# First attention of a macaron block: score products of the two-head fills on 32-row strips

## The reference

```python
Q = to_heads(x @ Wq); K = to_heads(x @ Wk); V = to_heads(x @ Wv)   # 16 heads of 8 features
scores = jnp.einsum('bhqd,bhkd->bhqk', Q, K) * scale
scores = jnp.where(causal_mask, -1000000.0, scores)
weights = jax.nn.softmax(scores, axis=-1)
attn = jnp.einsum('bhqk,bhkd->bhqd', weights, V)
```

## Time and profile before

| what | value |
|---|---|
| three runs, median (lowest to highest) | 2415.77 us (2415.32 to 2420.69) |
| profiled execution, its time | 2419.18 us |
| its span from the first to the last instruction | 2417.4 us |
| mean granted TensorE clock | 0.965 |
| busy: PE, PEld, DVE, ACT, POOL | 2228.5, 1476.6, 1759.1, 1448.1, 947.4 us |
| score products by query, 512 (L675): PE first and last start | 414.1 and 804.0 us |
| score products by key, 512 (L697): PE first and last start | 429.4 and 818.2 us |

### The profile page before, as it was taken

The page is one execution under the profiler, slowest core; times in us unless marked ns, Lnnn a source line. Parts: engine busy times, 40 slices in busy tenths (PEclk is TensorE's granted clock), DMA queues, the critical chain, the costliest instruction groups (busy, mean ns, idle before and its releaser), DMA issues.

```text
span 2417.4 us, 46156 instructions
## 1 busy us (share of the span) xinstructions
PE 2228.5 (92%) x11168; PEld 1476.6 (61%) x11168; DVE 1759.1 (73%) x3588; ACT 1448.1 (60%) x2256; POOL 947.4 (39%) x903
## 2 busy tenths in 40 slices
PE   2999998999999989999999999998989889999999
PEld 2666666666666666666667777763323337676666
DVE  4676675766777567666678887876767787778887
ACT  3655654554555555656576766665556556666666
POOL 1554454222232345555544444442121234444443
PEclk9999999999999999999999999998989899999999
DMA  3000002233222000000000000012323200000000
GB/s 144 1 0 0 0 0 61 62 89 96 85 78 72 16 12 13 13 9 11 14 1 1 0 0 0 0 46 78 105 78 99 83 1 5 5 4 4 4 4 9
DMA packets 59566, 78.93 MB, mean 33 GB/s; under 512 B 22784, under 2 KB 27104, under 8 KB 59232
## 3 DMA queue, kind: packets, MB, share of 16 engines
q1 hardware_dynamic: 59488, 77.99, 10.6%
HBM read 48.08 MB, written 29.88 MB: 32 GB/s over the span
## 4 chain that ended last, share of the span: by engine, by line
PE 55%; issue 17%; DVE 12%; POOL 11%; ACT 2%; DVEq 1%; DMA 1%; POOLq 0%; SPq 0%; ACTq 0%
PE pair L371 11%; POOL h_lo L1277 10%; PE pair L373 9%; PE pair L372 9%; PE pair L754 3%; PE bank L574 3%; PE pair L675 3%; PE pair L697 3%; PE bank L560 3%; PE pair L574 3%; PE pair L656 1%; PE bank L371 1%; DVE rmax L1110 1%; PE pair L684 1%; PE bank L373 1%
## 5 line engine op out<-in xcount | busy, mean ns | idle before, releaser
L1283 POOL TENSOR_TENSOR h_lo<-hid,h_hi 128x512 fp32r<-128x512 f32 x256 | 349.6, 1366 | 505.6 <-ACT h_hi L842 505.4
L1277 POOL TENSOR_TENSOR h_lo<-hid,h_hi 128x512 fp32r<-128x512 f32 x272 | 351.4, 1292 | 365.5 <-ACT h_hi L804 364.7
L371 PE MATMUL pair<-xnT_hi,w_hi 128*128 (+1 forms) x1056 | 484.4, 459 | 2.0 <-POOL w_lo L1275 1.2
L836 ACT ACTIVATE hid<-pair,bias 128x512 f32<-128x512 f32 x512 | 352.0, 688 | 181.5 <-PE pair L373 165.9
L372 PE MATMUL pair<-xnT_lo,w_hi 128*128 (+1 forms) x1056 | 421.6, 399 | 0.0
L373 PE MATMUL pair<-xnT_hi,w_lo 128*128 (+1 forms) x1056 | 420.3, 398 | 0.0
L371 PE MATMUL pair<-h_hi,w_hi 128*128 128x512 f32 x784 | 328.5, 419 | 40.6 <-DVE h_lo L1052 26.2
L372 PE MATMUL pair<-h_lo,w_hi 128*128 128x512 f32 x784 | 311.7, 398 | 0.0
L373 PE MATMUL pair<-h_hi,w_lo 128*128 128x512 f32 x784 | 311.7, 398 | 0.0
L1050 DVE CAST h_hi<-hid 128x512 fp32r<-128x512 f32 x256 | 193.1, 754 | 144.9 <-ACT hid L836 143.5
L804 ACT ACTIVATE h_hi<-hid 128x512 fp32r<-128x512 f32 x272 | 171.6, 631 | 176.5 <-DVE hid L1042 162.2
(11 more groups left out here) (177 smaller groups left out, 3669.3 us busy)
## 6 DMA issues: line engine op xcount, KB each, us to landing
parts_dram<-attn_parts SPq DMA_DIRECT2D x96, 256.0 KB, 2.9
attn_q_st<-parts_dram SPq DMA_DIRECT2D x64, 256.0 KB, 2.7
k_one<-parts_dram SPq DMA_DIRECT2D x128, 64.0 KB, 2.4
attn_k_st<-parts_dram SPq DMA_DIRECT2D x32, 256.0 KB, 3.0
stage_w<-in_w_dram SPq DMA_DIRECT2D x32, 130.0 KB, 2.1
stage_w<-in_w_dram SPq DMA_DIRECT2D x6, 512.0 KB, 12.6
x<-in_x_dram SPq DMA_DIRECT2D x1, 2048.0 KB, 7.8
mixed_dram<-attn_aT SPq DMA_DIRECT2D x32, 64.0 KB
```

The costliest lines, as they stand in the source:

```text
L371: eng.matmul(o, w_hi_, v_hi, start=start, stop=False, **kw)
L836: eng.activation(hid[:, j % NHID, :], bank[j % 3][:, :], ACT.Relu, bias=bias[:, B1 + j:B1 + j + 1]).then_inc(hid1_ready, 1)
L1277: eng.tensor_tensor(h_lo[:, p % NH0, :], hid[:, p % NHID, :], h_hi[:, p % NH0, :].bitcast(F32), ALU.subtract).then_inc(lo_ready, 1)
L1283: eng.tensor_tensor(h_lo[:, j % NH1, :], hid[:, j % NHID, :], h_hi[:, j % NH1, :].bitcast(F32), ALU.subtract).then_inc(lo1p_ready, 1)
```

## The change

A helper `strip(fill, j)` gives all 128 rows for fill 4 and the 32 rows of head j for fills 0 to 3. Both operands of both score products take these rows. The zeros of `k_one` are then not read in fills 0 to 3, and the result is the same sum. The numbers of instructions, their order, their waits and the banks that they write are as before; 12 of the 16 score products of a quad by query, and 12 of 16 by key, have 32 rows in place of 128, and the two heads of such a fill lie on neighbouring strips.

```diff
+        def strip(fill, j):
+
+            return slice(0, P) if fill == NF - 1 else slice(PC * j, PC * (j + 1))
+
         def scores_by_query(eng, ch, f, b):
...
             for j in heads_in(fill):
                 at0 = 256 * (j // 2) if fill == NF - 1 else 0
+                rows_ = strip(fill, j)
                 for i, (qt, at) in enumerate(Q_FILLS[fill][1]):
                     w, at = (qt + 1) * P, at + at0
-                    eng.matmul(pair[b][:, j % 2, at:at + w], mem0.q_st[:, quad, qt * P:(qt + 1) * P],
-                               mem0.k_one[:, quad, j, 0:w], start=(i == 0 and at0 == 0), stop=True, skip_group_check=True)
+                    eng.matmul(pair[b][:, j % 2, at:at + w], mem0.q_st[rows_, quad, qt * P:(qt + 1) * P],
+                               mem0.k_one[rows_, quad, j, 0:w], start=(i == 0 and at0 == 0), stop=True, skip_group_check=True)
...
         def scores_by_key(eng, ch, f, b):
...
             for j in heads_in(fill):
                 at0 = 256 * (j // 2) if fill == NF - 1 else 0
+                rows_ = strip(fill, j)
                 for i, (kb, at) in enumerate(K_FILLS[fill][1]):
                     w, at = S - kb * P, at + at0
-                    ins = eng.matmul(pair[b][:, j % 2, at:at + w], mem0.k_one[:, quad, j, kb * P:(kb + 1) * P],
-                                     mem0.q_st[:, quad, kb * P:S], start=(i == 0 and at0 == 0), stop=True, skip_group_check=True)
+                    ins = eng.matmul(pair[b][:, j % 2, at:at + w], mem0.k_one[rows_, quad, j, kb * P:(kb + 1) * P],
+                                     mem0.q_st[rows_, quad, kb * P:S], start=(i == 0 and at0 == 0), stop=True, skip_group_check=True)
             ins.then_inc(st_ready, 1)
```

## The result

The changed kernel takes 2466.70 us (median of four runs, 2463.44 to 2471.30), before 2415.55 us in the same comparison. The ratio is 1.0209, 95% interval 1.0187 to 1.0231: **slower by 51 us**. The prediction said 2486 us, slower, because TensorE's clock would fall in attn0. The page's row of busy times hides it: TensorE is busy 92% of the span as before, now of 2465.9 us.

What follows compares the result with a forecast made beforehand. TensorE's queue was taken to bound attn0. From the profiled 2419.2 us, -2 for the queue and +72 for the clock gave 2489, or 2486 us as a median; range 2412 to 2550.

Steps and rivals of the forecast that it cites:

- TensorE's queue bounds attn0: In attn0, TensorE's own queue sets the pace, except for one wait of up to 2.2 us for VectorE.
- wait of L704: TensorE's only large wait in attn0, once a chunk, read as for VectorE's maxima: 16.3 us in 370.
- Strips run side by side at full speed: From attn1's four 24-row products in 0.44 us: a two-product fill's second product runs beside the first, 0.23 us saved.
- Four-product fills, 0.12 us taken: Q2, Q3, K2 and K3 in attn0: each fill saves 0.12 us, 0.48 us a quad (0.16 to 1.16).
- case of program order: In a four-product fill, products start only in code order: 0.42 us in place of 0.57, 0.15 saved.
- upper bound of 0.29: In a four-product fill, the second head runs fully beside the first: 0.29 us saved of 0.57.
- Queue net -2 us: TensorE's queue in attn0: shape costs less strip gains, -4.5 us over 32 quads, half of gains taken: -13 to +6.
- Changes of shape: TensorE switching between strips and full rows: 0.09 us if a bf16 load follows, 0.18 if a float32r load follows.
- 1.26 us a quad: Cost in attn0 of switching between strips and full rows: 0.90 at fills plus 0.36 around inserted full-row steps.
- The clock holds less on few rows: A microsecond of products on few rows holds TensorE's clock up less than on all rows; forecast's chance 0.65.
- Its size, +72 us: Clock term in attn0: low-clock share 0.4 makes a chunk 58.6 us, +9.0, so +72 us for eight.
- ends of the clock term: Low-clock share 0.24, attn1's, gives +35 us; share 0.6 gives +128 us; stated as 2445 to 2550 us.

Runs made afterwards that it cites:

- three runs with full-row products at that place: Unread 512-column products added once a chunk: eight in the changed kernel, 2459.67 us; seven in the kernel before, 2431.73; seven with strips only in scores_by_query, 2418.30.
- By query alone: Changed kernel with scores_by_key back on all 128 rows, strips only in scores_by_query: 2415.36 us, ratio 0.9995 against the kernel before.
- 64-row run: Changed kernel with both heads of fills 0 to 3 on the 64 rows in which they lie: 2477.43 us, ratio 1.0266 against the kernel before.
- pair of extra products: Changed kernel plus eight unread 512-column products once a chunk at the same place: on 128 rows 2459.67 us, on 32 rows 2492.90 us.
- its halves: Changed kernel with strips kept only in scores_by_query, 2415.36 us, ratio 0.9995, or only in scores_by_key, 2428.77 us, ratio 1.0052, against the kernel before.
- tables of before: Unchanged step tables; other runs spread VectorE's steps to later slots: kernel before 2413.21 us, strips only in scores_by_query 2418.37, changed kernel 2453.32.
- K0 and K1 alone: Strips only in the two-product fills of scores_by_key, all other score products on 128 rows: 2418.58 us, ratio 1.0017 against the kernel before.

## Why the prediction was right, point by point

- **TensorE's queue bounds attn0.** Right: VectorE and ScalarE work as long as before, and a chunk follows TensorE's clock. The wait of L704 was misread in its cause: it is for the bank pair of Q0, not for the new maxima. The sum doesn't hang on that, but the three runs with full-row products at that place missed their forecasts with it.
- **Strips run side by side at full speed.** Right, from attn1's row, and across fills too, which the sum left out: at 630.33 four products on four strips, where the prediction has "at best two at a time".
- **Four-product fills, 0.12 us taken, near the case of program order.** The term was mis-sized: the fill takes 0.44 us to the mask instead of 0.57, with 0.09 for the change of shape in it, so 0.22 are saved, between the middle and the upper bound of 0.29. (The 0.04 of exposed load in these bounds has no row of its own.) Products of different strips overtake each other. The Trainium skill (TensorE: Matmul & The Clock Gate, Part 3) has products start in strict program order; the rows at 634.04 don't agree.
- **Queue net -2 us, bounds -13 to +6.** Carried back to full clock, 1.3 us a chunk, 10 us over eight chunks: near the lower bound. By query alone it is 1.0 to 1.3 us a chunk, measured at equal clock.
- **Changes of shape.** No run times one alone. That they cost something fits the 64-row run, 2.5 us a chunk with little gained, but the slower sequence of products on the same rows is in that too. The 1.26 us a quad stay unproven.
- **The clock holds less on few rows.** Right, and now shown by the pair of extra products, 33 us apart. The stretches of the earlier trace rows were weaker ground than the prediction took them for: the one of attn1 also holds products on column strips (1772.04 in the earlier trace rows). The Trainium skill (TensorE: Matmul & The Clock Gate, Part 1) has the clock follow how busy TensorE has been. By that the two runs of the pair would have the same clock; they have 0.83 and 0.74, and the measurement decides.
- **Its size, +72 us.** The share of the low clock in a chunk was taken as 0.4 and measured as 0.46; each microsecond of it was priced at 0.44 and costs 0.36; chunks at full clock take an estimated 47.1 us and not 48.3. A chunk takes 56.2 us and not 58.6: +6.6 and not +9.0, 53 us and not 72 for eight. That is about the 19 us by which the median was forecast too high. The errors cancel in part, and that is luck: by the prediction's own formula the larger share alone gives 16 us more, the lower price then takes some 21 off and the shorter chunk some 12. The price may be lower because part of the low clock lies over waits, which it doesn't lengthen; no run tests that. And the ends of the clock term, 2445 to 2550, should be 2449 to 2542 by their own terms; the measured time lies in both.
- **Open:** why the loss isn't the sum of its halves (0 and 13 us against 51). The traces show that low stretches last longer on few rows (13.7, 34.1 and 41.0 us at the start of the stage) and that, with the tables of before, only the two sets of strips together bring falls away from the long wait, four a chunk and not one. Why it takes both is open: no run puts a set number of strip products between full-row ones.

## What to carry to other kernels

A product whose unused rows are zero isn't only waste: here its full rows held TensorE's clock up. Before small products are packed on strips, read the granted clock of a stage that already does so, and count what the queue gains against what the clock gives back; packing only some of the products was neutral here (by query alone, or K0 and K1 alone) or cost little (7 to 13 us). And before filling a wait, find out which buffer it is for: work put behind it is only paid for.

## What was unexpected in the hardware

- Products on different strips overtake each other: the 384-column products of four heads in two fills start within 0.02 us, the 128-column ones 0.49 us later, though the code has them in between.
- 64 useless full-row products, 15 us of work at full clock and more at the low one, didn't make the changed kernel slower (2459.7 against 2466.7 us); the same on 32 rows cost 26 us.
- Products on 64 of 128 rows already bring the clock down: 0.88 against 0.96, with no more waiting than before, and for 41 us at the start of the stage it stayed at 0.50 with TensorE busy 38.9 of them.
